# Causal attention of a fused five-stage kernel: scores from q and k of a head pair instead of from x and K^T Q

## The reference

```python
q = jnp.einsum('qdh,bcd->bhcq', Q, x) * sq      # DQ = 64, D = 128, 16 heads, sq = sqrt(64/128)
k = jnp.einsum('qdh,bcd->bhcq', K, x) * sq
att = jnp.einsum('bhcq,bhCq->bhcC', q, k) / d_query
att = jnp.where(causal, att, -jnp.inf)
p = jax.nn.softmax(att, axis=-1)
y = jnp.einsum('bhcC,bhCv->bhcv', p, v)
```

## Time and profile before

| | |
|---|---|
| median of three runs | 1414.1 us (1413.49 to 1416.06) |
| profiled execution: span | 1415.4 us |
| profiled execution: time of its own beside the span | none is listed; the span stands for it |
| TensorE matmul busy | 1344.6 us, 95% |
| TensorE weight load busy | 1091.3 us, 77% |
| VectorE, ScalarE, GpSimd busy | 1023.0, 963.8, 588.3 us |

### The profile page before, as it was taken

The page is one execution under the profiler, slowest core; times in us unless marked ns, Lnnn a source line. Parts: engine busy times, 40 slices in busy tenths (PEclk is TensorE's granted clock), DMA queues, the critical chain, the costliest instruction groups (busy, mean ns, idle before and its releaser), DMA issues.

```text
span 1415.4 us, 36065 instructions
## 1 busy us (share of the span) xinstructions
PE 1344.6 (95%) x9787; PEld 1091.3 (77%) x9795; DVE 1023.0 (72%) x4813; ACT 963.8 (68%) x3377; POOL 588.3 (42%) x913
## 2 busy tenths in 40 slices
PE   5799977999999999999999999999999999999996
PEld 4688766878878787878787878787878787878884
DVE  6877789677777777777777777777777777777774
ACT  4644467577777777777777777777777777777774
POOL 5722157244444444444444444444444444444433
PEclk9999999899999999999999999999999999999999
DMA  7000000000000000000000000000000000000000
GB/s 199 1 1 0 1 1 1 0 2 2 2 9 0 8 0 8 0 8 0 8 0 8 0 8 0 8 0 8 0 8 0 8 0 8 0 8 0 9 1 16
DMA packets 14363, 12.29 MB, mean 9 GB/s; under 512 B 709, under 2 KB 12522, under 8 KB 14058
## 3 DMA queue, kind: packets, MB, share of 16 engines
q1 hardware_dynamic: 14240, 11.19, 3.0%
q10 hardware_dynamic: 10, 0.00, 0.0%
HBM read 7.00 MB, written 4.19 MB: 8 GB/s over the span
## 4 chain that ended last, share of the span: by engine, by line
PE 83%; DVE 6%; issue 4%; POOL 2%; ACT 1%; DMA 1%; SPq 1%; DVEq 0%; POOLq 0%; ACTq 0%
PE ps L1057 13%; PE ps L1040 12%; PE ps L1066 9%; PE ps L1007 4%; PE ps L1009 4%; PE ps L1008 4%; PE ps L1046 4%; PE ps L1029 4%; PE ps L1028 4%; PE ps L1030 4%; PE ps L1047 2%; PE ps L1048 2%; PE ps L1022 2%; PE ps L1021 2%; PE ps L1020 2%
## 5 line engine op out<-in xcount | busy, mean ns | idle before, releaser
L314 POOL TENSOR_TENSOR pr<-pr,rinv 128x256 f32<-128x256 f32 x256 | 157.5, 615 | 665.5 <-DVE rinv L517 665.5
L745 ACT ACTIVATE pr<-ps,neg_max 128x128 f32<-128x128 f32 (+1 forms) x1024 | 425.0, 425 | 0.0
L509 DVE CUSTOM_DVE_ANT_0 ps<-ps,mask 128x128 f32<-128x128 f32 (+1 forms) x1024 | 335.2, 387 | 0.0
L316 POOL TENSOR_TENSOR pr<-pr,rinv 128x512 f32<-128x512 f32 x256 | 266.7, 1042 | 0.0
L493 DVE TENSOR_TENSOR u_lo<-ps,u_hi 128x512 fp32r<-128x512 f32 x256 | 176.8, 691 | 101.9 <-ACT u_hi L731 101.1
L1057 PE MATMUL ps<-pT,space 128*64 128x256 f32 (+1 forms) x2048 | 222.9, 339 | 15.3 <-DVE pT L524 15.3
L1057 PEld LDWEIGHTS ps<-pT,space 128*64 128x64 f32 x2048 | 124.2, 136 | 146.6 <-issue 60.6
L1040 PE MATMUL ps<-ident,pr 128*128 128x128 f32 x1536 | 218.0, 275 | 1.5 <-POOL pr L316 1.4
L745 ACT ACTIVATION_READ_ACCUMULATOR pr<-ps,neg_max 128x1 f32 x1024 | 211.4, 206 | 0.0
L1040 PEld LDWEIGHTS ps<-ident,pr 128*128 128x128 f32 x1536 | 176.2, 140 | 33.4 <-issue 12.3
L769 ACT COPY space<-ps 128x256 f32<-128x256 f32 x256 | 95.8, 374 | 145.3 <-PE ps L1057 145.3
(11 more groups left out here) (171 smaller groups left out, 2645.8 us busy)
## 6 DMA issues: line engine op xcount, KB each, us to landing
out<-x_all SPq DMA_DIRECT2D x16, 256.0 KB, 2.3
x_all<-L_attn_x SPq DMA_DIRECT2D x1, 768.0 KB, 6.3
x_all<-L_attn_x SPq DMA_DIRECT2D x1, 512.0 KB, 4.1
space<-L_attn_Q SPq DMA_DIRECT2D x1, 512.0 KB, 15.7
space<-L_attn_K SPq DMA_DIRECT2D x1, 512.0 KB, 9.8
space<-L_attn_V SPq DMA_DIRECT2D x1, 512.0 KB, 11.4
space<-L_attn_W SPq DMA_DIRECT2D x1, 512.0 KB, 12.0
dft_s<-dft SPq DMA_DIRECT2D x1, 192.0 KB, 2.5
```

What stands on the lines that cost most here:

```text
L316: nc.gpsimd.tensor_tensor(pr[:, j, :, 1:3, :].rearrange("p h b k -> p h (b k)"), pr[:, j, :, 1:3, :].rearrange("p h b k -> p h (b k)"), r[ ...
L509: last = nc.vector.tensor_tensor_reduce(o, o, mask[:, T - w:T], -1.0, -MASKED, ALU.add, ALU.min, neg_max[:, j, 2 * h + qt:2 * h + qt + 1])
L745: last = nc.scalar.activation(dst, ps[:, BANK_S + 2 * j + qt, h * w:(h + 1) * w], ACT.Exp, bias=neg_max[:, j, at:at + 1], scale=-1.0, accu ...
```

## The change

g is gone. From the loaded Q and K, transposes make `wqk`, the 128x64 weights of all heads for q and for k, split in high and low. `qk_product` makes q and k of a pair: 128 output rows are the two heads' 64 rows each, with the 256 tokens as columns, one half of the bank for q and one for k; again six matmuls of 256 moving columns. The scores contract over the 64 rows of one head: per head and `qt` three matmuls with 128 or 256 moving columns, twelve in a step. All of head 0 come first (array rows 0 to 63), then all of head 1 (rows 64 to 127), and each head has its own PSUM bank. Masking and exponentials go by head accordingly.

```diff
-            def g_weights():
+            def qk_weights():
                 pe.wait_ge(in_qk, 32)
...
-                    last = mm(ps[:, h // 4, (h % 4) * D:(h % 4 + 1) * D], k_h[:, h, :], q_h[:, h, :], start=True, stop=True)
+                for i in range(4):
+                    raw = (q_raw, k_raw)[i // 2].rearrange("q (d h) -> q h d", h=H)
+                    for h in range(H // 2):
+                        last = tr(ps[:, i, h * DQ:(h + 1) * DQ], raw[:, (i % 2) * (H // 2) + h, :], ident[0:DQ, 0:DQ])
+                    last.then_inc(su_pe, 1)
...
-            def u_product(n, h2, jb, j):
-                for k in range(2):
-                    h = 2 * h2 + k
-                    o = ps[:, BANK_U, k * T:(k + 1) * T]
-                    mm(o, g_hi[:, h, :], x_hi[:, jb, :], start=True, stop=False, skip_group_check=True)
-                    mm(o, g_hi[:, h, :], x_lo[:, jb, :], start=False, stop=False, skip_group_check=True)
-                    last = mm(o, g_lo[:, h, :], x_hi[:, jb, :], start=False, stop=True, skip_group_check=True)
-                last.then_inc(u_done, 1)
+            def qk_product(n, p, jb, j):
+                of_pair = slice(p * 2 * DQ, (p + 1) * 2 * DQ)
+                for s in range(2):
+                    o = ps[:, BANK_QK, s * T:(s + 1) * T]
+                    mm(o, wqk_hi[:, s, of_pair], x_hi[:, jb, :], start=True, stop=False, skip_group_check=True)
+                    mm(o, wqk_hi[:, s, of_pair], x_lo[:, jb, :], start=False, stop=False, skip_group_check=True)
+                    last = mm(o, wqk_lo[:, s, of_pair], x_hi[:, jb, :], start=False, stop=True, skip_group_check=True)
+                last.then_inc(qk_done, 1)
...
             def scores(n, jb, j):
-                pe.wait_ge(ulo_ready, count(n + 1))
-                if above_0(2 * n - 3):
-                    pe.wait_ge(exp_ready, count(2 * n - 3))
-                o = ps[:, BANK_S + 2 * j, 0:2 * P].rearrange("p (h k) -> p h k", h=2)
-                uh, ul = (a[:, j, :, 0:P] for a in (u_hi, u_lo))
-                xh, xl = x_hi[:, jb, 0:P], x_lo[:, jb, 0:P]
-                mm(o, xh, uh, start=True, stop=False, skip_group_check=True)
-                mm(o, xh, ul, start=False, stop=False, skip_group_check=True)
-                mm(o, xl, uh, start=False, stop=True, skip_group_check=True).then_inc(s_done, 1)
+                pe.wait_ge(qklo_ready, count(n + 1))
                 if above_0(2 * n - 2):
                     pe.wait_ge(exp_ready, count(2 * n - 2))
-                o = ps[:, BANK_S + 2 * j + 1, :].rearrange("p (h k) -> p h k", h=2)
-                uh, ul = u_hi[:, j], u_lo[:, j]
-                xh, xl = x_hi[:, jb, P:2 * P], x_lo[:, jb, P:2 * P]
-                mm(o, xh, uh, start=True, stop=False, skip_group_check=True)
-                mm(o, xh, ul, start=False, stop=False, skip_group_check=True)
-                mm(o, xl, uh, start=False, stop=True, skip_group_check=True).then_inc(s_done, 1)
+                for h in range(2):
+                    of_head = slice(h * DQ, (h + 1) * DQ)
+                    for qt in range(2):
+                        w = (qt + 1) * P
+                        for k, (q, key) in enumerate(((qk_hi, qk_hi), (qk_hi, qk_lo), (qk_lo, qk_hi))):
+                            last = mm(ps[:, BANK_S + 2 * j + h, qt * P:qt * P + w], q[of_head, j, 0, qt * P:(qt + 1) * P],
+                                      key[of_head, j, 1, 0:w], start=(k == 0), stop=(k == 2), skip_group_check=True)
+                    last.then_inc(s_done, 1)
...
             def mask_scores(n, j):
-                dve.wait_ge(s_done, count(2 * n + 1))
                 if above_0(2 * n - 2):
                     dve.wait_ge(exp_ready, count(2 * n - 2))
-                for qt in range(2):
-                    w = (qt + 1) * P
-                    if qt == 1:
-                        dve.wait_ge(s_done, count(2 * n + 2))
-                    nc.vector.memset(pause[:, 2 * j + qt:2 * j + qt + 1], 0.0)
-                    for h in range(2):
-                        o = ps[:, BANK_S + 2 * j + qt, h * w:(h + 1) * w]
+                for h in range(2):
+                    dve.wait_ge(s_done, count(2 * n + (1 + h)))
+                    nc.vector.memset(pause[:, 2 * j + h:2 * j + h + 1], 0.0)
+                    for qt in range(2):
+                        w = (qt + 1) * P
+                        o = ps[:, BANK_S + 2 * j + h, qt * P:qt * P + w]
```

More of the change, by code:

```diff
@@ L141, in build @@
         rest = sb("rest", [1, 2, 4 * D])
-        g_hi = sb("g_hi", [P, H, D], F32R); g_lo = sb("g_lo", [P, H, D], F32R)
+        wqk_hi = sb("wqk_hi", [P, 2, H * DQ], F32R); wqk_lo = sb("wqk_lo", [P, 2, H * DQ], F32R)
         v_hi = sb("v_hi", [P, H * DV], F32R); v_lo = sb("v_lo", [P, H * DV], F32R)
@@ L166, in build @@
         x_hi = sb("x_hi", [P, 2, T], F32R); x_lo = sb("x_lo", [P, 2, T], F32R)
-        u_hi = sb("u_hi", [P, 2, 2, T], F32R); u_lo = sb("u_lo", [P, 2, 2, T], F32R)
+        qk_hi = sb("qk_hi", [P, 2, 2, T], F32R); qk_lo = sb("qk_lo", [P, 2, 2, T], F32R)
         neg_max = sb("neg_max", [P, 2, 4]); rsum = sb("rsum", [P, 2, 4]); rinv = sb("rinv", [P, 2, 4])
@@ L190, in build @@
         den_ready = sem("den_ready"); zr_ready = sem("zr_ready"); y0_ready = sem("y0_ready"); y0t_done = sem("y0t_done"); yT0_ready = sem("yT0_ready")
-        u_done = sem("u_done"); uhi_ready = sem("uhi_ready"); ulo_ready = sem("ulo_ready")
+        qk_done = sem("qk_done"); qkhi_ready = sem("qkhi_ready"); qklo_ready = sem("qklo_ready")
         s_done = sem("s_done"); max_ready = sem("max_ready"); exp_ready = sem("exp_ready")
@@ L219, in build @@
         V_BANKS, W_BANKS = (4, 7), (0, 6)
-        BANK_U, BANK_S, BANK_X, BANK_T = 0, 1, 5, 6
+        BANK_QK, BANK_S, BANK_X, BANK_T = 0, 1, 5, 6
         FIRST_V_BANKS = (BANK_X, BANK_T, BANK_T + 1, BANK_X)
@@ L237, in build @@
         V_TURN = 4
+        QK_SCALES = (SCORE_SCALE, 1.0)
         @block.sync
@@ L487, in x_low, with qk_low @@
                 nc.vector.tensor_tensor(x_lo[:, j, :], ps[:, BANK_X, 0:T], x_hi[:, j, :].bitcast(F32), ALU.subtract).then_inc(xlo_ready, 1)
-            def u_low(n, j):
-                dve.wait_ge(uhi_ready, count(n + 1))
+            def qk_low(n, j):
+                dve.wait_ge(qkhi_ready, count(n + 1))
                 if above_0(2 * n - 2):
                     dve.wait_ge(s_done, count(2 * n - 2))
-                nc.vector.tensor_tensor(u_lo[:, j].rearrange("p h k -> p (h k)"), ps[:, BANK_U, :],
-                                        u_hi[:, j].rearrange("p h k -> p (h k)").bitcast(F32), ALU.subtract).then_inc(ulo_ready, 1)
+                nc.vector.tensor_tensor(qk_lo[:, j].rearrange("p s k -> p (s k)"), ps[:, BANK_QK, :],
+                                        qk_hi[:, j].rearrange("p s k -> p (s k)").bitcast(F32), ALU.subtract).then_inc(qklo_ready, 1)
             def mask_scores(n, j):
-                dve.wait_ge(s_done, count(2 * n + 1))
                 if above_0(2 * n - 2):
                     dve.wait_ge(exp_ready, count(2 * n - 2))
-                for qt in range(2):
-                    w = (qt + 1) * P
-                    if qt == 1:
-                        dve.wait_ge(s_done, count(2 * n + 2))
-                    nc.vector.memset(pause[:, 2 * j + qt:2 * j + qt + 1], 0.0)
-                    for h in range(2):
-                        o = ps[:, BANK_S + 2 * j + qt, h * w:(h + 1) * w]
+                for h in range(2):
[4 more added lines that the diff above has]
+                        o = ps[:, BANK_S + 2 * j + h, qt * P:qt * P + w]
                         last = nc.vector.tensor_tensor_reduce(o, o, mask[:, T - w:T], -1.0, -MASKED, ALU.add, ALU.min,
@@ L555, in z_norm, with qk_weights_low @@
                 last.then_inc(z_xn_ready, 1)
-            def g_low():
+            def qk_weights_low():
                 for i in range(4):
                     dve.wait_ge(su_hi, count(i + 1))
-                    nc.vector.scalar_tensor_tensor(out=g_lo[:, 4 * i:4 * i + 4, :].rearrange("p h d -> p (h d)"),
-                                                   in0=ps[:, i % 4, :], scalar=SCORE_SCALE,
-                                                   in1=g_hi[:, 4 * i:4 * i + 4, :].rearrange("p h d -> p (h d)").bitcast(F32),
+                    at = slice(512 * (i % 2), 512 * (i % 2) + 512)
+                    nc.vector.scalar_tensor_tensor(out=wqk_lo[:, i // 2, at], in0=ps[:, i, :], scalar=QK_SCALES[i // 2],
+                                                   in1=wqk_hi[:, i // 2, at].bitcast(F32),
                                                    op0=ALU.mult, op1=ALU.subtract).then_inc(su_lo, 1)
@@ L574, in _ @@
             ln_soft_norm(0, 0)
-            g_low()
+            qk_weights_low()
             x_low(0, 0)
             v_low()
-            u_low(0, 0)
-            u_low(1, 1)
+            qk_low(0, 0)
+            qk_low(1, 1)
             mask_scores(0, 0)
-            u_low(2, 0)
+            qk_low(2, 0)
```

(64 more changed lines are left out.)

## The result

The changed kernel takes 1434.61 us (1433.75 to 1436.47, 4 runs) against 1414.99 us (1413.49 to 1416.06, 4 runs): a ratio of 1.014, 95% interval [1.0125, 1.0154], +20 us.

A forecast was written before the change was run, and what follows sets the result against it. TensorE's instruction queue was taken to bound the attention; +0.35 +0.09 -0.05 = +0.39 us a step, x 256 = +101, less 12 and 3, gives +86 us: 1500 us. Its own range was 1450 to 1560, the whole range 1440 to 1700.

The forecast's parts named there:

- narrow matmuls: Scores: 128-column matmuls cost their weight load, 0.105 to 0.1175 us each; twelve matmuls 1.41 us for 1.06, +0.35 a step.
- second half beside the first: Scores, change from head 0's rows to head 1's: the two halves overlap briefly, -0.05 us a step.
- What bounds the kernel: Attention stretch: a queue of TensorE instructions, extra time per step paid 256 times, at most 17 us of real lateness.
- The switch: One more tile shape change per step, whole array to half rows before the scores: +0.09 us, bounds 0 and 0.20.
- Only the last matmul of head 0 and the first of head 1 are neighbours, so this can gain 0.1175 at most: Scores, between heads: only one neighbouring pair can overlap; gain at most 0.1175 us, cost 0.105 if the load isn't ahead.
- Loads follow one another on one path: Scores: weight loads queue singly, 128 columns take about 0.105 us, so a narrow matmul costs its load.
- The others: VectorE, ScalarE and set-up: 12 us given back from late `pT` waits, 3 us saved in set-up transposes.
- A: Rival, scores: narrow float32r matmuls cost the plain float32 price, 0.235 us for 128 columns; 1675 us, chance 0.17.
- B: Rival, scores: loads don't hide within one row half, +1.30 us a step; 1727 us, chance 0.07.
- C: Rival, not slower: 64-row loads take half the time, 0.052 us, narrow matmuls 0.059; 1404 us, chance 0.13.
- D: Rival, attention stretch: 64-row matmuls make the granted clock fall to 0.5; over 2250 us, chance 0.02.
- My argument from L868: Set-up transposes, 16 with 64-row weights in 2.04 us, 0.115 apart at clock 0.5: loads are hidden within the same rows.

The follow-up runs named there:

- e3: Changed kernel with its twelve score matmuls contracting over all 128 rows, without halves, same columns and order: 1477.5 us.
- e4: Changed kernel with both heads' score matmuls on rows 0 to 63, so no second half to work beside: 1527.9 us.
- e1: Changed kernel with the twelve score matmuls of a step alternating between head 0 and head 1: 1377.6 us, ratio 0.9741 to the kernel before.

## Why the forecast was wrong

Per step, in us, with the kernels that isolate each term:

| term | forecast | measured | by |
|---|---|---|---|
| narrow matmuls | +0.35 | +0.318 | e3 less before |
| half rows: gap and second load | +0.09 | +0.197 | e4 less e3 |
| second half beside the first | -0.05 | -0.402 | changed less e4 |
| sum | +0.39 | +0.113 | |

**What bounds the kernel** was right: steps went from 4.126 to 4.237 us (medians, first matmul of `u_product` or `qk_product` to the next), 256 x 0.111 = 28 us.

**Narrow matmuls** were right, though no row had shown one: the load's 52 ns for 64 more columns gave their price.

**The switch** was half right. Its entry costs 0.092, as forecast. I had seen the second part as well, the uncovered load of 0.105 after `products`, and set it to the way back, as a bound of 0.20. It comes at every switch, behind the first matmul: 0.10 us going into the scores and into `values` (L1046), 0.05 to 0.06 going into `products` and into transposes, whose loads are busy 0.14 us, not 0.19.

**"Only the last matmul of head 0 and the first of head 1 are neighbours, so this can gain 0.1175 at most"** is the step that failed. It assumed that matmuls start in the program's order. The gain is 0.402, and I had made its bound a hard one, so that even the range missed. The row against it was among those I read. In L1057 the order is both passes of one head, then both of the other, first with 256 columns, then with 128. Neighbours alone could save 0.235 + 0.1175 + 0.1175 = 0.47 of 1.41 and leave 0.94; the block takes 0.80 with its switch. The price of 0.235 was the one of 512 float32r columns; these passes start 0.216 and 0.109 us apart, and that still leaves 0.87. The trace of the kernel before shows the order itself: the first two passes start 7 ns apart, so they are one of each head, though the program has two passes of one head in a row. The view merges these two passes, each 0.43 us long, in one row:

```profile
903.35 0.44 PE L1057 MATMUL ps<-pT,space 128*64 128x256 f32 x2
```

I took it as "two halves run at once" and did not put the difference from 0.94 to the account of order. "Loads follow one another on one path" goes with it: that holds within a half (starts 0.11 to 0.12 apart in e4), and the two halves load side by side (e1). The Trainium skill says, in "TensorE: Matmul & The Clock Gate", Part 3, that matmuls are strictly in order and only loads are pulled ahead. The trace differs for different row or column halves: the seventh matmul starts 0.104 us before the fourth. The Trainium skill, "TensorEngine Tiling (Array Packing)", section "Tiling Modes", says that tiles operate independently, with loads and matmuls in parallel, and the two starts of a pair in e1, 3 ns apart, agree.

**That it is slower at all** is owed to the second half of the switch. Without it the measured terms are 0.318 + 0.092 - 0.402 = +0.008 a step, 2 us. Two of my errors pulled in opposite ways, so the right direction was in part luck.

**The others** had the right sign. From the first step to the last the attention takes 23 us more than before, so 5 of the 28 are given back (forecast 12 of a larger loss). They come where `products` waits less for `pT`: between the first score matmul and `products`, the time above the median falls from 32 us in all to 26. The first matmul of `qk_product` starts 4.7 us earlier than that of `u_product` did, 0.9 of which were gained before the set-up; forecast 3. No wait for exponentials worth a microsecond arose (0.4 us in all).

**The rivals.** A and B are refuted by e3 and e4. C was nearest in time, and not for its reason: a load isn't faster with 64 rows (0.11 apart in e4). D didn't occur; the clock is 1.00 in the attention from 281 us on. None of my rivals had matmuls out of order, which is what happened.

## What to carry to other kernels

Matmuls on different halves of the array run side by side, and the order in the queue decides for how long. In these runs the idle half was served when no more than three matmuls of the busy half were left in front. Work for two halves should therefore alternate in short runs: one, three and four in a row were about equally good here, six were not, and five was not tried. With that the same twelve matmuls cost 0.89 us instead of 1.17, and the change that was 20 us slower is 36 us faster. When a block takes less time than your model of it allows, even by 0.1 us, the model lacks a mechanism, and no bound can be taken from it.

## What was not expected of the hardware

Matmuls overtake one another across row halves (0.104 us in the changed kernel), and in L1057 across column halves. Right after a change of tile shape a load stays uncovered behind the first matmul, 0.105 us ahead of the scores, besides the gap of 0.092. And 64-row transposes with weights 64 bytes apart start 0.11 to 0.12 us apart at either clock: 32 in 3.78 us at a granted clock of 1.00 in the changed set-up, 16 in 2.04 us at 0.5. The clock that slows other matmuls does not slow these, so their spacing doesn't tell whether loads are hidden. My argument from L868 was weaker than I made it; e4 gave the answer. The rows behind it, set-up of the changed kernel:

```profile
259.30 3.78 PE L858 MATMUL ps<-ident,space 64*128 64x64 f32 x32
```
